# Two attentions and two feed-forwards on one core: second attention in the stage of its queries, rows moved sooner

## The chip, the cores and the metric

The kernel is one program for one core of a Trainium2 chip. The metric is the device time of an execution in microseconds (us), lower being better. All times below are of this one core. Its engines are TensorE (PE, with PEld for its weight loads), VectorE (DVE), ScalarE (ACT), GpSimd (POOL), and SyncE (SP), which here only issues transfers (DMA).

## What is computed

The reference runs two layers on `x` (8 batches, 112 rows, 512 wide) and a context of 8 x 375 rows:

```python
x = x + attention0(layernorm(x), context)     # one head, softmax(x c^T / sqrt(512)) c, masked
x = x + ffn0(layernorm(x))                    # rmsnorm, 8-bit activations, ternary w1, w2, w3, silu gate, 1408 wide
x = x + layernorm(Wo attention1(layernorm(x), context)) * gamma + beta   # 16 heads of 32, scaled
x = x + ffn1(layernorm(x))                    # integer weights 1408 wide with row scales, silu gate
```

The keys and values of attention1 are products of the context with `Wk` and `Wv` and hang on nothing of `x`. Products in f32 are made of two parts each (high and low), so every such product is three matmuls. The scores of attention1 are clipped to -50..50 (after the exponential, as a clip of `e`).

## The kernel before

All 896 rows are 7 tiles of 128 rows for the feed-forwards, and 8 batches of 112 rows for the attentions. The program is a row of blocks, one per stage; in each, every engine has its own list of instructions, written out by hand, and waits only on semaphores. Between two blocks stands a barrier: no engine begins the next block before all five have ended theirs.

- **First stage** (0 to 142 us): attention0 for each batch b, with the first 31 of 56 pieces of the keys and values of attention1 (`kv_product`, L161 to L180, pieces in the order k, k, v, k, v, k, v of each batch) woven between. SP stores every piece (`kv_spill`). For batch b, DVE's `add(b)` (L767) raises `x1_ready`, and SP's `move(b)` (L347) copies the 112 rows from `x` (by batch) to `xres` (by tile) with one or two DMAs. SP issues in order, so a move also waits for all that stands ahead of it. For b = 6 DVE's `tile_statistics(0)` (L441) waits until the rows of batches 0 to 5 have landed. The ternary form of w1 and w2 is made here by POOL (`scale_weight`, L322) and DVE (`ternary_weight`, L329 and L330); the last half of w2 is DVE's last work in this block.
- **Second stage** (142 to 271 us): ffn0 tile by tile with the other 25 pieces. It begins with the transposes of the first two tiles (`turn_input`, L1100), which share a PSUM bank, so that the second waits for ACT's copy of the first (L959). Three gate and up products (`gate_up`, L1109) per tile follow, with pieces 31 to 37 between those of tiles 0 and 1. ACT adds up |w3| in two halves (`sum_weight`, L301), PE totals them (`total_weight`, L308), DVE inverts, POOL scales, DVE rounds.
- **Queries** (the end of the same block, 264 to 297 us): seven transposed tiles, then `query(n, g)` (L1183): four groups g of heads for tiles 0 to 2 (n = 0) and for tiles 3 to 6 (n = 1), each 12 matmuls into the PSUM bank of its group (the same four banks for both n). ACT and DVE read it (L1061, L1340), and `q_lo` counts what DVE has done. `queries_stack(n)` (L877) waits for 4(n+1) of these and issues 8 DMAs which lay the queries of all heads in `qst`. Set 0 is stacked here, and SP waits for its landing before the block ends. The keys and values of batches 0 and 1 are fetched into `kst` and `vst` here too (L229, L234).
- **Second attention** (a block of its own, 297 to 395 us): `scores(m)` (L1617) for m = 0 to 31, which is group m % 4 of batch m // 4, 12 matmuls; ACT's exponential (L1574), DVE's clip (L1672), `values(b, g)` (L1631, L1634). PE works two groups of scores ahead of the values. SP begins with `queries_stack(1)`, then fetches the keys of batch b + 2 once the scores of batch b are done (`s_sum`), the values once its values are done. Scores of batch 3 and later need set 1 of the queries, the others set 0.
- **The rest** (398 to 517 us): ffn1 and the output.

## Time and profile before

| | us |
|---|---|
| three timed runs: median (lowest, highest) | 523.45 (521.83, 1657.42) |
| profiled execution, its time | 518.96 |
| its span, first to last instruction | 517.2 |
| TensorE busy in the span | 473.5 |
| VectorE, ScalarE, GpSimd busy | 293.4, 248.9, 84.0 |

The highest of the three is an outlier that nothing in the profile accounts for. All timeline numbers are microseconds from the start of the profiled execution's span; 1.8 us of its time lie outside the span. TensorE being busy 92% of the span makes every stop of it a candidate for the end, so a change is read off at the places where PE stands still.

### The profile page before, as it was taken

How to read it: one execution, taken by the hardware profiler on the slowest of the kernel's cores; microseconds unless marked ns; L12 is line 12 of the kernel's file. 1: busy time of each engine (PE TensorE's matmuls, PEld its weight loads, DVE VectorE, ACT ScalarE, POOL GpSimd, SP SyncE). 2: the span in 40 equal slices, each digit the busy share in tenths (PEclk: the TensorE clock that was granted, in tenths of full speed). 3: DMA queues.
4: the chain of work that ended last, by engine and by line, in shares of the span. 5: the costliest groups of instructions: out<-in, count | busy, mean ns of one | idle time of the engine just before them, and what ended most of it. 6: DMA issues, size and time to landing. Idle time of an engine off the chain costs nothing. (4 is left out here: it accounts for less than half of the span.)

```text
span 517.2 us, 10260 instructions
## 1 busy us (share of the span) xinstructions
PE 473.5 (92%) x4018; PEld 358.1 (69%) x4018; DVE 293.4 (57%) x554; ACT 248.9 (48%) x373; POOL 84.0 (16%) x105
## 2 busy tenths in 40 slices
PE   3899999999598799999997889999996998999997
PEld 3778888877376566666767677778874654555996
DVE  4674364428846956655564235668885686555211
ACT  4545433553357365666564287857761575112000
POOL 2210400024024000000108001133332116000000
PEclk9999999999979999999999989999999999999999
DMA  8989586923572113111127599777601546000011
GB/s 279 352 303 374 188 287 211 324 64 121 151 283 96 52 36 113 37 51 41 49 95 328 122 192 372 268 234 241 212 4 31 173 124 182 0 0 1 35 53 53
DMA packets 42716, 79.30 MB, mean 153 GB/s; under 512 B 5553, under 2 KB 30129, under 8 KB 40369
## 3 DMA queue, kind: packets, MB, share of 16 engines
q1 hardware_dynamic: 42672, 78.69, 46.1%
q8 instruction: 30, 0.49, 0.4%
q14 instruction: 12, 0.10, 0.0%
q10 hardware_dynamic: 2, 0.01, 0.0%
HBM read 58.76 MB, written 14.42 MB: 141 GB/s over the span
## 5 line engine op out<-in xcount | busy, mean ns | idle before, releaser
L179 PE MATMUL psum<-wv_p,kv_p 128*128 128x512 f32 x288 | 75.5, 411 | 6.5 <-DVE khl L199 5.1
L177 PE MATMUL psum<-kv_p,wk_p 128*128 128x384 f32 x384 | 75.8, 348 | 1.9 <-DVE khl L199 1.3
L177 PEld LDWEIGHTS psum<-kv_p,wk_p 128*128 128x128 f32 x384 | 68.3, 193 | 4.1 <-issue 2.9
L179 PEld LDWEIGHTS psum<-wv_p,kv_p 128*128 128x128 f32 x288 | 53.3, 188 | 23.1 <-issue 11.6
L1574 ACT ACTIVATE e<-psum,mask_bias 128x448 f32<-128x448 f32 x96 | 53.7, 636 | 14.8 <-PE psum L1617 14.6
L199 DVE SCALAR_TENSOR_TENSOR khl<-psum,bqk,khl 128x384 f16<-128x384 f32 x32 | 19.7, 616 | 44.0 <-ACT khl L189 43.9
L1844 PE MATMUL psum<-xt,wg_b 128*128 128x448 f16 x176 | 36.9, 352 | 3.1 <-DVEq L1919 3.1
L1631 PE MATMUL psum<-e,vst 128*32 128x112 f32 x768 | 37.7, 267 | 2.0 <-DVE e L1672 1.8
L1672 DVE TENSOR_SCALAR e<-e 128x1344 f32<-128x1344 f32 x32 | 28.2, 881 | 16.3 <-ACT e L1574 16.3
L1844 PE MATMUL psum<-xt,wu_b 128*128 128x448 f16 x176 | 36.9, 352 | 0.0
L1893 PE MATMUL psum<-h_p,wd_r 128*128 x176 | 36.0, 366 | 0.0
L193 ACT ACTIVATE vsp<-psum 128x512 f32<-128x512 f32 x24 | 14.3, 597 | 43.2 <-PE psum L179 42.9
L1893 PEld LDWEIGHTS psum<-h_p,wd_r 128*128 128x128 f32 x176 | 33.1, 188 | 2.7
L189 ACT ACTIVATE khl<-psum,bqk 128x384 f16<-128x384 f32 x32 | 18.4, 579 | 31.4 <-PE psum L177 31.4
L1790 ACT ACTIVATE gate<-psum,gs 128x448 f32<-128x448 f32 x22 | 13.9, 631 | 38.0 <-PE psum L1844 35.9
L1844 PEld LDWEIGHTS psum<-xt,wg_b 128*128 (+1 forms) x176 | 17.1, 98 | 18.6 <-issue 3.4
L322 POOL TENSOR_SCALAR w_stage<-w_stage,w_stat 128x2816 f32<-128x2816 f32 x6 | 16.4, 2738 | 80.8 <-DVE w_stat L317 80.7
L1907 DVE SCALAR_TENSOR_TENSOR hf<-psum,sgu,gate 128x448 f32<-128x448 f32 x22 | 15.0, 683 | 24.8 <-ACT gate L1790 24.8
L1617 PE MATMUL psum<-qst,kst 128*128 128x112 f16 x384 | 25.2, 215 | 3.8 <-PEq L1371 1.8
L1844 PEld LDWEIGHTS psum<-xt,wu_b 128*128 (+1 forms) x176 | 17.2, 98 | 16.1
L1617 PEld LDWEIGHTS psum<-qst,kst 128*128 128x128 f16 x384 | 20.0, 99 | 9.6 <-issue 5.8
L1634 PE MATMUL psum<-e,z_pick 128*32 128x112 f32 x512 | 25.1, 263 | 0.6 <-issue 0.6
(188 smaller groups left out, 834.7 us busy)
## 6 DMA issues: line engine op xcount, KB each, us to landing
kst<-k_scratch SPq DMA_DIRECT2D x8, 1536.0 KB, 8.2
kv_raw<-in_ctx_feat SPq DMA_DIRECT2D x12, 768.0 KB, 5.0
w_stage<-in_w SPq DMA_DIRECT2D x6, 1408.0 KB, 7.9
cn<-in_ctx_tok SPq DMA_DIRECT2D x8, 768.0 KB, 7.5
k_scratch<-khl SPq DMA_DIRECT2D x128, 48.0 KB, 1.7
v_scratch<-vsp SPq DMA_DIRECT2D x24, 256.0 KB, 2.2
vst<-v_scratch SPq DMA_DIRECT2D x8, 768.0 KB, 6.4
wd_int<-in_wd SPq DMA_DIRECT2D x11, 256.0 KB, 3.8
```

Of the source, the lines that this page charges most:

```text
L177: mm = pe.matmul(psum[:, kv_bank(p), 0:TP], wk_p[:, u, k, n * P:(n + 1) * P], src[:, v, k, :], **ends)
L179: mm = pe.matmul(psum[:, kv_bank(p), :], src[:, u, k, n * P:(n + 1) * P], wv_p[:, v, k, :], **ends)
L189: act.activation(khl[n][:, 0, :], psum[:, kv_bank(p), 0:TP], ACT.Identity, bias=bqk[:, 1, n:n + 1]).then_inc(kv_hi, 1)
L199: dve.scalar_tensor_tensor(khl[n][:, 1, :], psum[:, kv_bank(p), 0:TP], bqk[:, 1, n:n + 1], khl[n][:, 0, :], ALU.add, ALU.subtract).then_in ...
L322: pool.tensor_scalar(w_stage[:, w_half_of[half]], w_stage[:, w_half_of[half]], w_stat[:, 4 * n + 2:4 * n + 3], ROUND, ALU.mult, ALU.add).t ...
L1574: act.activation(e[g][:, c, :], psum[:, D_S + (TC * g + c) % 4, 0:4 * S], ACT.Exp, bias=mask_bias[:, b, c:c + 1]).then_inc(e_raw, 1)
L1617: mm = pe.matmul(psum[:, D_S + (TC * g + c) % 4, hh * S:(hh + 1) * S], kst[b % 2][:, g, hh, c * P:(c + 1) * P], qst[:, g, hh, b * S:(b + 1 ...
L1631: mm = pe.matmul(psum[32 * hh:32 * hh + 32, D_UZ[b][0], g * S:(g + 1) * S], vst[b % 2][:, c, (4 * g + hh) * HD:(4 * g + hh + 1) * HD], e[g ...
L1634: mm = pe.matmul(psum[32 * hh:32 * hh + 32, D_UZ[b][1], 0:S], (z_pick_last if c == TC - 1 else z_pick)[:, g, :], e[g][:, c, hh * S:(hh + 1 ...
L1672: dve.tensor_scalar(e[g][:], e[g][:], EXP_LOW, EXP_HIGH, ALU.max, ALU.min).then_inc(e_ready, 1)
L1844: mm = pe.matmul(psum[:, F_GU + 2 * q + m, 0:HALF], w[:, k, bass.ts(j, P)], xt[:, u, k, a * HALF:(a + 1) * HALF], start=(k, u) == (0, 0), ...
L1893: mm = pe.matmul(psum[:, F_D + m, 0:HALF], wd_r[:, j, m * P:(m + 1) * P], h_p[:, a, u, j, :], start=(j, u) == (0, 0), stop=(j, u) == (JC - ...
```

## The change

1. **First stage.** SP's `move(b)` stands ahead of the last pieces of batch b (`A_KV[b][2]`), no longer behind them at the start of batch b + 1. `ternary_weight(1, 1)` leaves the end of DVE's list and stands near the start of its list in the second block; PE's first `gate_up` waits for it, and so does SP's load of the second half of w3.
2. **Start of the second stage.** The second transpose has a bank of its own (`input_bank`) and waits for nothing of ACT. ACT's second `sum_weight` of w3 moves behind `square(0, 0)` and `normalized(6)`, PE's `total_weight` behind piece 34. DVE's and POOL's small steps around it change places, and one tiny scale of `row_scale` moves into `add`.
3. **Queries and second attention are one block.** The barrier between them goes. `query(1, 0)` and `query(1, 1)` use two other banks and wait for none of the first set's reads. `scores(0)` stands between `query(1, 1)` and `query(1, 2)`, `scores(1)` between `query(1, 2)` and `query(1, 3)`; `scores(0)` waits for the landing of stack 0, SP no longer does. ACT's exponentials and DVE's clips are woven in the same way. `wq_p1` moves to other memory so that `e` can be written earlier.

```diff
@@ first stage, SP, batch b
-                if b:
-                    move(sp, b - 1)
                 for p in A_KV[b][0]:
...
                     load_tok(b + 3)
+                move(sp, b)
                 for p in A_KV[b][2]:
@@ DVE, end of the first stage and start of the second
             input_integers(dve, 1)
-            ternary_weight(dve, 1, 1)
...
             gate_scales(1, 1)
+            ternary_weight(dve, 1, 1)
             keys_values((31,))
@@ second stage, PE
-                after(pe, xqt_ready, t)
+                after(pe, xqt_ready, t if t != 1 else 0)
...
             keys_values((31,))
+            pe.wait_ge(w_ternary, 4)
             gate_up(0, 0, 0)
@@ SP, end of the queries
             queries_stack(sp, 0)
-            sp.wait_ge(q_stacked[0], STACK)
+            queries_stack(sp, 1)
+            for b in range(B):
+                if b + 2 < B:
+                    sp.wait_ge(s_sum, TC * G * (b + 1))
+                    keys_fetch(sp, b + 2, b % 2)
...
@@ PE, queries and scores
-        C_T, C_Q = 0, 2
+        C_T, C_Q = 0, ((2, 3, 4, 5), (6, 7, 4, 5))
...
-                after(pe, q_lo, G * (n - 1) + g + 1)
+                if n == 1 and g < 2:
+                    pe.wait_ge(x2_ready, TILES + 1)
+                    kv_wait_read(pe, NP * B - 1)
+                if n == 1 and g >= 2:
+                    pe.wait_ge(q_lo, g + 1)
...
-            for g in range(G):
-                query(1, g)
+            query(1, 0)
+            query(1, 1)
+            scores(0)
+            query(1, 2)
+            scores(1)
+            query(1, 3)
@@ PE, scores(m), and values(b, g) for g == 0
-                    if b == 3:
-                        pe.wait_ge(q_stacked[1], STACK)
+                    if b in (0, 3):
+                        pe.wait_ge(q_stacked[b // 3], STACK)
+                if m < 2:
+                    pe.wait_ge(c_lo, TILES)
+                    pe.wait_ge(q_lo, m + 1)
...
+                    if b < 2:
+                        pe.wait_ge(ones_set, 6)
+                        pe.wait_ge(q_lo, G + 2 * (b + 1))
```

How the lists read at three places. First, SP in the first stage, batch 5 (`xres<-x` is the move of rows, `v_scratch` and `k_scratch` are pieces 23 and 24). Before:

```order
L208 DMA k_scratch<-khl_76 32x2x384 [waits kv_left]
L208 DMA k_scratch<-khl_76 32x2x384 x3
L211 DMA v_scratch<-vsp 128x512 [waits kv_hi]
L208 DMA k_scratch<-khl_77 32x2x384 [waits kv_left]
L208 DMA k_scratch<-khl_77 32x2x384 x3
L347 DMA xres<-x 80x512 [waits x1_ready]
L347 DMA xres<-x 32x512
```

Now:

```order
L208 DMA k_scratch<-khl_76 32x2x384 [waits kv_left]
L208 DMA k_scratch<-khl_76 32x2x384 x3
L347 DMA xres<-x 80x512 [waits x1_ready]
L347 DMA xres<-x 32x512
L211 DMA v_scratch<-vsp 128x512 [waits kv_hi]
L208 DMA k_scratch<-khl_77 32x2x384 [waits kv_left]
L208 DMA k_scratch<-khl_77 32x2x384 x3
```

The move of batch 5 has gone ahead of pieces 23 and 24, for which it had waited.

Second, ACT at the start of the second stage (`w3q,w_stat` is the second half of |w3|, `hy,hstat` the square of tile 0, `xn_b` a normalized tile, `khl` and `vsp` pieces 33 and 34). Before:

```order
L967 ACTIVATE silu_112<-psum,hstat 128x512
L301 ACTIVATE w3q,w_stat<-w_stage 128x2816
L458 ACTIVATE xn_b<-xres,bstat,rstd 128x512
L189 ACTIVATE khl_78<-psum,bqk 128x384
L967 ACTIVATE silu_111<-psum,hstat 128x384
L458 ACTIVATE xn_b<-xres,bstat,rstd 128x512
L974 ACTIVATE hy,hstat<-hid_105 128x1408
L193 ACTIVATE vsp<-psum 128x512
```

Now:

```order
L1151 ACTIVATE silu_112<-psum,hstat 128x512
L462 ACTIVATE xn_b<-xres,bstat,rstd 128x512
L189 ACTIVATE khl_78<-psum,bqk 128x384
L1151 ACTIVATE silu_111<-psum,hstat 128x384
L1158 ACTIVATE hy,hstat<-hid_105 128x1408
L462 ACTIVATE xn_b<-xres,bstat,rstd 128x512
L301 ACTIVATE w3q,w_stat<-w_stage 128x2816
L193 ACTIVATE vsp<-psum 128x512
```

The sum has moved from ahead of piece 33 to just ahead of piece 34's read; PE's total stands behind the product of piece 34.

Third, PE where the scores begin (`wq_p` and `xnt_p` are a query product, `qst,kst` scores). Before:

```order
L1183 MATMUL psum<-xnt_p_1615,wq_p_1611 128x512
L1371 UNCONDITIONAL_BRANCH
L1606 UNCONDITIONAL_BRANCH [waits barrier_Pool_Activation_PE_DVE_SP_release]
L1617 MATMUL psum<-qst,kst_80 128x112 [waits kst_loaded0]
L1617 MATMUL psum<-qst,kst_80 128x112 x15
```

Now:

```order
L1411 MATMUL psum<-xnt_p_1611,wq_p_1607 128x512
L1442 MATMUL psum<-qst,kst_80 128x112 [waits c_lo,q_lo,q_stacked0,kst_loaded0]
L1442 MATMUL psum<-qst,kst_80 128x112 x11
L1411 MATMUL psum<-xnt_p_1611,wq_p_1606 128x512 [waits hqt_ready,q_lo,c_lo,wq_lo]
L1411 MATMUL psum<-xnt_p_1611,wq_p_1606 128x512
```

The first scores stand in the middle of the query products, with a wait for stack 0 of their own, and the rest of the queries stands behind that wait.

## Rows read from the trace of the kernel before

**Rows 1.** The page: busy time of each engine.

```profile
PE 473.5 (92%) x4018; PEld 358.1 (69%) x4018; DVE 293.4 (57%) x554; ACT 248.9 (48%) x373; POOL 84.0 (16%) x105
```

**Rows 2.** Timeline, end of the first stage: start, us, work, [idle before <- what ended it].

```profile
106.97 0.75 DVE L767 SCALAR_TENSOR_TENSOR x<-psum,arow,x 112x512 f32<-112x512 f32 x1 [1.01 <-PE psum L703]
...
114.79 1.17 SPq L347 DMA_DIRECT2D xres<-x  x2
...
117.51 3.06 DVE L441 BATCH_NORM_STATS2 ln_stat<-xres 128x6 f32<-128x512 f32 x5 [4.24 <-DMA xres<-x]
...
128.11 2.32 PE L177 MATMUL psum<-kv_p,wk_p 128*128 128x384 f32 x12 [0.44 <-ACT vsp L193]
...
133.90 3.04 PE L179 MATMUL psum<-wv_p,kv_p 128*128 128x512 f32 x12 [0.90 <-DVE khl L199]
...
137.47 1.48 ACT L215 ACTIVATE kv_p<-kv_raw 128x1536 fp32r<-128x1536 f32 x1
138.40 0.54 DVE L482 TENSOR_SCALAR xs<-xres,ln_mv,bstat 128x512 f32<-128x512 f32 x1
...
140.97 0.89 DVE L330 TENSOR_SCALAR w2q<-w2q 128x2816 bf16<-128x2816 bf16 x1
```

**Rows 3.** Timeline, start of the second stage.

```profile
142.19 0.59 PE L1100 MATMUL psum<-ident_bf,xq 128*128 128x128 bf16 x4 [5.25 <-PEq L834]
...
143.89 4.00 PE L177 MATMUL psum<-kv_p,wk_p 128*128 128x384 f32 x12
...
154.86 2.54 ACT L301 ACTIVATE w3q<-w_stage 128x2816 bf16<-128x2816 f32 x1
...
159.47 3.04 PE L179 MATMUL psum<-wv_p,kv_p 128*128 128x512 f32 x12 [1.31 <-DVE khl L199]
...
160.80 2.63 POOL L322 TENSOR_SCALAR w_stage<-w_stage,w_stat 128x2816 f32<-128x2816 f32 x1 [5.66 <-DVE w_stat L317]
...
162.14 1.57 DVE L482 TENSOR_SCALAR xs<-xres,ln_mv,bstat 128x512 f32<-128x512 f32 x1
...
162.35 1.04 PE L1109 MATMUL psum<-w1q,xqt 128*128 128x512 bf16 x4
...
184.75 3.14 PE L179 MATMUL psum<-wv_p,kv_p 128*128 128x512 f32 x12
```

**Rows 4.** Timeline, queries and first scores (SPq: issue of a DMA).

```profile
284.27 11.15 PE L1183 MATMUL psum<-xnt_p,wq_p 128*128 128x512 f32 x48 [1.53 <-issue]
...
290.22 0.61 SPq L877 DMA_DIRECT2D qst<-qhl  x1
...
296.18 0.75 DVE L1340 SCALAR_TENSOR_TENSOR qhl<-psum,bqk,qhl 128x512 f16<-128x512 f32 x1 [1.97 <-ACT qhl L1061]
...
297.22 1.26 SPq L877 DMA_DIRECT2D qst<-qhl  x2
297.26 0.95 PE L1617 MATMUL psum<-qst,kst 128*128 128x112 f16 x16 [1.84 <-PEq L1371]
...
306.09 1.55 SPq L229 DMA_DIRECT2D kst<-k_scratch  x1
...
316.13 0.76 PE L1617 MATMUL psum<-qst,kst 128*128 128x112 f16 x12 [0.37 <-DMA kst<-k_scratch]
```

**Rows 5.** SP's waits, 280 to 300 us; landing of the key fetch of 306.09.

```profile
SPq L1371 <- DMA qst<-qhl: 3.2, 1, 3.2
...
kst<-k_scratch SPq DMA_DIRECT2D x1, 1536.0 KB, 10.0
```

**Rows 6.** Stretches: us, busy (count) of PE, PEld, DVE, ACT, POOL, clock, DMA, GB/s.

```profile
142.00:148.00 6.00, 5.04 (x22) 4.56 (x23) 0.21 (x2) 1.27 (x3) 0.00 (x0) 0.54 1.03 376
301.00:304.50 3.50, 3.35 (x60) 2.70 (x57) 1.89 (x3) 2.35 (x5) 0.00 (x0) 0.52 1.02 223
316.00:317.00 1.00, 0.87 (x20) 0.79 (x24) 0.75 (x1) 0.41 (x1) 0.00 (x0) 1.00 0.99 403
395.00:398.00 3.00, 0.01 (x1) 0.00 (x0) 2.44 (x5) 0.00 (x0) 0.10 (x1) 1.00 0.00 0
```

More of the change, by code:

```diff
@@ L1371, in build @@
-        part.close()
         e = [at(f"e{r}", [P, TC, 4 * S], F32, 56576 + r * 5376) for r in range(4)]
@@ new lines, in _ @@
+            turned_input(0, 0)
+            turned_input(1, 1)
+            keys_values((31,))
+            sum_weight(act, 2, 0)
+            gate(0, 0, 0)
+            keys_values((32,))
+            gate(0, 0, 1)
+            normalized(act, 5)
+            keys_values((33,))
+            gate(0, 0, 2)
+            square(0, 0)
+            normalized(act, 6)
+            sum_weight(act, 2, 1)
+            keys_values((34,))
+            gate(1, 1, 0)
+            scaled(0, 0)
+            keys_values((35,))
@@ new lines, in _, with tile_normalized @@
+            gate(1, 1, 1)
+            turned_input(2, 0)
+            keys_values((36,))
+            gate(1, 1, 2)
+            keys_values((37,))
+            turned_hidden(0)
+            keys_values(B_KV[0][0])
+            square(1, 1)
+            gate(2, 0, 0)
+            scaled(1, 1)
+            split_feat(act, B_SLOT[2], B_FILL[2])
+            for t in range(TILES - 2):
+                step(t, t % 2)
+            def tile_normalized(t):
+                act.wait_ge(b_shift, 3 if t < TILE_SETS[0][1] else 4)
+                after(act, c_turned, t - 1)
+                act.activation(xn_c[:, t % 2], xres[:, t, :], ACT.Identity, scale=rstd[:, t], bias=bstat[:, 7, t]).then_inc(c_xn, 1)
@@ new lines, in down, with step @@
+            def down(t):
+                pe.wait_ge(w_ternary, 6)
+                pe.wait_ge(hqt_ready, t + 1)
+                pe.wait_ge(x2_ready, t + 1)
+                for j in range(JC):
+                    mm = pe.matmul(psum[:, B_DN, :], hqt[:, j, :], w3q[:, j, :], start=j == 0, stop=j == JC - 1)
+                mm.then_inc(down_sum, 1)
+            def step(t, q):
+                gates, inputs = t + 2 < TILES, t + 3 < TILES
+                turn_hidden(t)
+                keys_values(B_KV[t][0])
+                if gates:
+                    gate_up(t + 2, q, 0)
+                down(t)
+                keys_values(B_KV[t][1])
+                if gates:
+                    gate_up(t + 2, q, 1)
+                if inputs:
+                    turn_input(t + 3)
+                keys_values(B_KV[t][2])
+                if gates:
+                    gate_up(t + 2, q, 2)
@@ new lines, in _, with turn @@
+            gate_up(1, 1, 2)
+            keys_values((37,))
+            for t in range(TILES - 1):
+                step(t, t % 2)
+            def turn(t):
+                pe.wait_ge(c_xn, t + 1)
+                pe.wait_ge(up_read, 3 * TILES)
+                after(pe, c_lo, t - 1)
+                if t == QT[0][1]:
+                    pe.wait_ge(kv_sum, NP * B)
+                for k in range(KC):
+                    mm = pe.transpose(psum[:, C_T + t % 2, k * P:(k + 1) * P], xn_c[:, t % 2, k * P:(k + 1) * P], ident[:])
+                mm.then_inc(c_turned, 1)
@@ L1608, in scores @@
+            turn_hidden(6)
+            keys_values(B_KV[6][0])
+            turn(0)
+            turn(1)
+            down(6)
+            turn(2)
+            turn(3)
+            query(0, 0)
+            turn(4)
+            query(0, 1)
+            query(0, 2)
+            turn(5)
+            query(0, 3)
+            turn(6)
             def scores(m):
```

793 lines of the change are left out of this document (353 added, 440 removed).

## The prediction, made before the changed kernel was run

> **What bounds the kernel now.** I read the page first: TensorE is busy for 473.5 of 517.2 us [rows 1], so 44 us are its stops, and only a stop, or TensorE's clock, can give or cost time. Then I read TensorE's timeline at the three places that the change touches, looking for each stop and for what ended it.
>
> At the end of the first stage TensorE has stopped at 136.94 (133.90 + 3.04) and begins again at 142.19, after 5.25 us [rows 2, 3]. The last engine to end that block is DVE, at 141.86 (140.97 + 0.89), with the ternary weights [rows 2]. DVE is late because it stood for 4.24 us until 117.51 for moved rows: the rows of batch 5 were ready at 107.72 (106.97 + 0.75), but their move was issued at 114.79 only [rows 2]. The same lag makes TensorE wait 0.44 and 0.90 us at 128.11 and 133.90 [rows 2].
>
> In the second stage the pieces and gate products are nearly dense; one stop of 1.31 us stands at 159.47, since ACT spent 2.54 us on |w3| ahead of piece 33 [rows 3].
>
> Between the queries and the scores TensorE stands for 1.84 us [rows 4] and then runs its first scores and values thinly, partly at the lower clock [rows 6]. This looks like the loss to remove. But the scores that begin at 316.13 (the first of batch 2) waited 0.37 us for their keys [rows 4]. So up to there the time is set by another chain: last query read by DVE at 296.93 (296.18 + 0.75), barrier, eight stack DMAs from 297.22, key fetch issued at 306.09, landed 10.0 us later, at 316.1 [rows 4, 5]. What TensorE does between is beside it.
>
> **The change part by part.** I write the new times on the clock of the old trace.
>
> *Rows sooner, first stage.* The move of batch 5 can be issued at 107.8 and lands by about 111 (the old one, issued at 114.79, had landed at 117.5 [rows 2]). DVE is ready for it at 113.27 (117.51 - 4.24). The 4.24 us go from DVE, though not all reach the stage's end, since some of its next steps wait for TensorE; I count 1.8 to 3.4 there. TensorE loses its two waits and ends piece 30 at 136.94 - 1.34 = 135.6.
>
> *The ternary half leaves the block.* DVE would end 2.54 us (1.65 + 0.89) sooner for that alone, at 139.4, and with the rows at 136.0 to 137.6. Now ACT is the last: its split of the next context began 0.53 us after TensorE's end and took 1.48, so it ends at 135.6 + 2.0 = 137.6 [rows 2]. With 0.3 for the barrier (141.86 to 142.19) the second stage begins at 138.0 to 138.2 in place of 142.19. I take -4.0; the ends are -1.9 (SP's last issues near 140.0 hold the barrier) and -5. The moved half costs 2.54 us of DVE in the next block, beside piece 31; TensorE's first gate product needs it 2.9 us in, and cannot start before 3 us in.
>
> *Start of the second stage.* The second transpose saves its wait of about 0.8 us. Piece 31 took 4.00 us at a granted clock of 0.54, that is mostly the lower one of 1.2 GHz [rows 3, 6]; a like piece at 2.4 GHz took 2.32 [rows 2]. If the shorter stop (2.4 us in place of 5.25) keeps the clock, another 1.7 us go. Counting on through gate products and pieces with the same durations, TensorE ends piece 34 at 16.3 us after its start. Here stands a new wait: the total of |w3|. ACT makes the square of tile 0 and a normalized tile first (until 16.9), then 2.54 us of sum and its read-out: 19.65. So TensorE stops for 3.3 us and its next gate product begins at 20.0, against 20.16 before (162.35 - 142.19). Then a shorter chain brings the two transposes' gain back, and DVE's third and fourth ternary steps, now later, hold piece 39: 40.4 against 42.56 (184.75 - 142.19). One thing eats of this: DVE's step at 162.14 took 1.57 us, ending 0.3 us after POOL's scaling of 160.80 to 163.43, where the same shape on its own took 0.54 [rows 2, 3]; now the rounding of tile 0 falls within POOL's second scaling, and waits some 1.3 us, which goes through to piece 36. I take -0.9; the ends are -2.2 (no such wait) and +1 (the clock stays low to piece 31).
>
> The Trainium skill (SBUF — State Buffer, "SBUF: two separate sides") says that VectorE and GpSimd share a port pair under an exclusive lock held for the whole instruction. The row at 162.14 agrees. Without the rule the sum would have -2.2 here in place of -0.9.
>
> *Queries and scores.* Up to query(1, 1) nothing changes: 284.27 plus half of 11.15 is 289.85. scores(0) then waits for stack 0. Its last DMA was issued at 290.22 and ended at 290.83, and SP waited 3.2 us more: landed at 294.0 [rows 4, 5]. So TensorE stops for 4.2 us, and the two last query products stand behind that wait. 0.76 of scores, 2.79, 0.76, 2.79: query(1, 3) ends at 301.1, ACT and DVE read it by 302.6 (0.7 + 0.75). Stack 1 hangs on this read and starts at 302.6 in place of 297.22: 5.4 us later. SP's queue behind it is as before, 8.9 us of issues and then the key fetch with 10.0 us. The keys land at 321.5 and scores of batch 2 begin 5.4 us later than before. The scores and values up to there run sooner, but only lengthen the stop ahead of it, to some 7 us. I take +5.4; the low end is +1.1 (were stack 0 there at 289.85, the two groups of scores alone delay the last query by 1.5, less 0.3 for the barrier), the high end is in the rivals.
>
> *The clock.* After 5.25 us of standing the clock was low [rows 3, 6]; after 3.05 us at 395 it was not (1.00), after the thin stretch from 295 it was, at 301 to 304.5 [rows 6]. The new stop of 7 us lies beyond the first case: I count 1.7 us, as piece 31 lost. The stop of 4.2 us lies between: 0.7 x 1.7 = 1.2, at the end of which every delay goes straight into the chain. For the 3.3 and the 2.4 us stops I count nothing.
>
> Behind batch 2 the order is the old one. The next keys were issued at 314.5 by the same queue and needed at 326.8; with all shifted they have more slack.
>
> Sum: -4.0 - 0.9 + 5.4 + 1.7 + 1.2 = +3.4. On the profiled execution's 518.96 that is 522.4, on the median of 523.45, which stands 4.5 above it (0.9%), 526.8. I predict 526.8.
>
> **The rivals.**
>
> *The attention gains what it shows.* If the chain of stack and keys had slack that I don't see, the merged block would give back its thin start: 1.84 of idle, some 2 us of thin scores and 1.1 of low clock (an estimate from 301 to 304.5 [rows 6]), 5 us. Then -4.0 - 0.9 - 5.0 = -9.9, and up to -12 with the clock kept in the second stage: 513.5 to 511.5. For it speak the idle rows; against it the 0.37 us wait at 316.13, which leaves no slack.
>
> *Clock.* TensorE falls to 1.2 GHz at each of the stops of 2.4, 3.3, 4.2 and 7 us. It decides if even the stop of 2.4 us ahead of the second stage brings the clock down. Against the sum that is 1.8 + 1.7 + 0.5 more: 530.8, slower than before by 7.4 us. For it speaks the thin stretch at 301, against it 395 to 398.
>
> *The key fetch shares.* Before, the values and `Wo` were issued 4.3 us behind the keys; now both stand ready behind them. If the three land together, 3.4 MB at the 403 GB/s of 316 us [rows 6] take 8.4 us. The last stack issue would end at 311.5 and land some 5 us later; the keys come at 325.0, 3.5 later: 530.3. The Trainium skill (DMA: Bandwidth & Descriptors, "Two DMAs through the same engine are not ordered") says that descriptors of one queue start in order, which speaks against it.
>
> *Rows sooner does nothing.* The barrier stays at 140 for SP's issues: -1.9 for -4.0, 528.9.
>
> **How the numbers follow.** The forecast (all within 3 us of 526.8) gets 0.43, the gaining attention 0.12, the clock 0.20, the sharing 0.12, the barrier 0.08, the rest 0.05. A measurement of this kernel tells about 2% (10.5 us) from no change. Below 513.0 lies a part of the first rival only, 0.05; above 533.9 clock and sharing together, 0.07; within 0.88. The range for 8 in 10 goes from 518, where the gaining attention meets the forecast's low end, to 533, where clock and sharing meet.
>
> **What would show it.** In the changed profile: DVE's wait for `xres` gone, and the second stage starting near 138.0; a stop of some 3.3 us at the total of |w3|, released by ACT; a stop near 4 us at the first scores, released by a DMA; stack 1 issued over 5 us later against query(1, 0), and a stop of about 7 us at the first scores of batch 2, released by `kst`, with the clock below 1.00 behind it. I am wrong if scores(0) finds stack 0 landed, if the keys of batch 2 are waited for less than 3 us, or if the first stage ends later than 140.

## The result and the profile after the change

The changed kernel takes 526.16 us (median of 6 runs, 524.31 to 527.22) and the kernel before, run beside it, 522.41 us. The ratio is 1.0084, with a 95% interval of 1.0048 to 1.012: slower by 2.5 to 6.3 us, 4.4 in the middle, and less than the 2% below which the prediction calls a difference no change. The profiled execution has a span of 524.9 us, 7.7 more than that of before. Why the profiles differ by more than the medians is part of the reading below.

The page, where [rows 1] stood before:

```profile
PE 479.4 (91%) x4018; PEld 362.1 (69%) x4018; DVE 292.7 (56%) x554; ACT 248.4 (47%) x373; POOL 82.5 (16%) x105
```

TensorE is busy for 5.9 us more with the same 4018 matmuls. Nothing was added to its work, so it ran some of it at the lower clock.

Timeline of the changed kernel at the end of its first stage, for [rows 2]:

```profile
107.42 0.75 DVE L769 SCALAR_TENSOR_TENSOR x<-psum,arow,x 112x512 f32<-112x512 f32 x1 [1.01 <-PE psum L705]
...
108.20 1.17 SPq L347 DMA_DIRECT2D xres<-x  x2
...
113.64 3.05 DVE L445 BATCH_NORM_STATS2 ln_stat<-xres 128x6 f32<-128x512 f32 x5
...
125.80 4.41 PE L177 MATMUL psum<-kv_p,wk_p 128*128 128x384 f32 x24
...
136.11 1.48 ACT L215 ACTIVATE kv_p<-kv_raw 128x1536 fp32r<-128x1536 f32 x1
...
137.78 0.61 SPq L211 DMA_DIRECT2D v_scratch<-vsp  x1
...
138.89 1.01 PE L1323 MATMUL psum<-ident_bf,xq 128*128 128x128 bf16 x8 [3.31 <-PEq L835]
```

The rows of batch 5 are moved 0.78 us after their addition began, where it was 7.8 us, and DVE's wait of 4.24 us for them is gone. TensorE's two small waits are gone too: what stood as two groups of 12 with 0.44 us between them is one of 24. The last to end the stage is SyncE, with a spill that ends at 138.39. The second stage starts 31.47 us after the addition of batch 5 began (138.89 - 107.42), where it was 35.22.

Start of the second stage, for [rows 3]:

```profile
156.24 2.53 ACT L301 ACTIVATE w3q<-w_stage 128x2816 bf16<-128x2816 f32 x1
...
158.92 0.81 PE L308 MATMUL psum<-w_stat,ones_f 128*128 128x1 f32 x4 [2.98 <-ACT w3q L301]
...
159.59 1.87 PE L1332 MATMUL psum<-w1q,xqt 128*128 128x512 bf16 x4
...
160.22 5.21 POOL L322 TENSOR_SCALAR w_stage<-w_stage,w_stat 128x2816 f32<-128x2816 f32 x2 [2.83 <-DVE w_stat L317]
...
161.25 1.70 PE L1332 MATMUL psum<-w2q,xqt 128*128 128x512 bf16 x4
...
165.20 0.97 DVE L1535 TENSOR_SCALAR hq<-hy 128x1408 bf16<-128x1408 f32 x1 [0.70 <-ACT hy L1163]
```

The new stop at the total of |w3| is there, 2.98 us long and ended by ScalarE. The gate product behind it takes 1.87 us, where a like one took 1.04 [rows 3].

Queries and first scores, for [rows 4]:

```profile
280.54 5.78 PE L1411 MATMUL psum<-xnt_p,wq_p 128*128 128x512 f32 x24 [1.53 <-issue]
...
290.28 1.28 PE L1442 MATMUL psum<-qst,kst 128*128 128x112 f16 x12 [3.96 <-issue]
...
291.33 5.03 PE L1411 MATMUL psum<-xnt_p,wq_p 128*128 128x512 f32 x12
...
300.55 0.75 DVE L1635 SCALAR_TENSOR_TENSOR qhl<-psum,bqk,qhl 128x512 f16<-128x512 f32 x1 [1.00 <-ACT qhl L1245]
...
310.64 0.66 SPq L229 DMA_DIRECT2D kst<-k_scratch  x1
...
319.02 1.30 PE L1442 MATMUL psum<-qst,kst 128*128 128x112 f16 x12 [5.99 <-DMA kst<-k_scratch]
```

Before, four query products ran as one row of 48 matmuls in 11.15 us. Now two run, TensorE stops for 3.96 us at scores(0), and the third product takes 5.03 us in place of 2.8. The last query is read at 301.30, that is 20.76 us after query(1, 0) began (12.66 before); the keys are issued 30.10 us after it (21.82 before); the scores of batch 2 begin 38.48 us after it (31.86 before), behind a stop of 5.99 us.

Stretches, for [rows 6] (us, busy (count) of PE, PEld, DVE, ACT, POOL, clock, DMA, GB/s):

```profile
160.00:164.00 4.00, 4.00 (x16) 2.32 (x15) 0.37 (x2) 0.97 (x2) 3.78 (x2) 0.68 0.79 262
290.00:294.00 4.00, 3.72 (x18) 3.21 (x19) 0.86 (x1) 1.68 (x3) 0.00 (x0) 0.50 0.00 0
316.00:324.00 8.00, 4.98 (x92) 4.39 (x96) 0.86 (x1) 2.41 (x5) 0.00 (x0) 0.57 1.01 421
440.00:442.00 2.00, 2.00 (x7) 0.89 (x6) 0.60 (x1) 0.00 (x0) 1.10 (x2) 0.50 0.72 217
```

Behind each of the stops of 2.98, 3.96 and 5.99 us the clock was at 1.2 GHz (0.50) for a while: 0.50 is that level, 0.68 and 0.57 are stretches of which it fills a part. One more such stretch, at 440, stands in the last stage, which the change does not touch, and another at the product that starts that stage, behind a stop as long as before:

```profile
401.97 3.12 PE L1844 MATMUL psum<-xt,wg_b 128*128 128x448 f16 x8 [3.06 <-DVEq L1919]
...
437.67 0.66 PE L998 MATMUL psum<-ident,xn_e 128*128 128x128 f32 x4 [2.16 <-ACT xn_e L975]
...
438.60 2.73 PE L1844 MATMUL psum<-xt,wg_b 128*128 128x448 f16 x8
```

In the profile of before that product began at 398.06 behind a stop of 3.05 us, took 1.67 us, and from 398 to 402 the clock was 1.00. From there to the end before took 119.1 us (517.2 - 398.06) and the changed kernel 122.9. So 3.8 of the 7.7 us between the two spans come from a stage with the same code. They can be told apart row by row: the first product is 1.45 us longer; behind the stop of 2.16 us (1.59 before) the two products that start at 438.60 (gate and up) take 4.71 us until the next begins, where the same two took 3.02; and that stop itself is 0.57 us longer. That is 3.1 us of lower clock and 0.6 of a longer wait.

### The profile page after: what moved, and what is told of

Same layout as the page of the kernel before. It is cut to its first block and busy times, and to the rows that moved or that the text cites. A ratio compares the mean times of both kernels' runs of the same rounds, so it can differ in the third digit from the quotient of the medians.

```text
span 524.9 us, 10260 instructions
## 1 busy us (share of the span) xinstructions
PE 479.4 (91%) x4018; PEld 362.1 (69%) x4018; DVE 292.7 (56%) x554; ACT 248.4 (47%) x373; POOL 82.5 (16%) x105
## 5 line engine op out<-in xcount | busy, mean ns | idle before, releaser
L1844 PE MATMUL psum<-xt,wg_b 128*128 128x448 f16 x176 | 39.4, 370 | 3.1 <-DVEq L1919 3.1
L1667 DVE TENSOR_SCALAR e<-e 128x1344 f32<-128x1344 f32 x32 | 28.2, 881 | 22.4 <-ACT e L1276 22.4
L1515 DVE SCALAR_TENSOR_TENSOR hid<-psum,bstat,silu 128x512 f32<-128x512 f32 (+1 forms) x21 | 14.8, 704 | 20.9 <-ACT silu L1151 20.6
```

Source lines behind the costliest of these rows:

```text
L1667: dve.tensor_scalar(e[g][:], e[g][:], EXP_LOW, EXP_HIGH, ALU.max, ALU.min).then_inc(e_ready, 1)
L1844: mm = pe.matmul(psum[:, F_GU + 2 * q + m, 0:HALF], w[:, k, bass.ts(j, P)], xt[:, u, k, a * HALF:(a + 1) * HALF], start=(k, u) == (0, 0), ...
```

## The experiments

Three times cut the span into what each part of the change can reach: from the addition of batch 5 to the second stage, from there to query(1, 0), and from there to the first gate product of the last stage. They are differences of starts in TensorE's timeline of each profile (the addition of batch 5 in DVE's). All ratios are to the kernel before, run beside, and a time in us that goes with one is worked out from it. Rows of one column with the same code show how far single profiles scatter: 30.5 to 31.9 us in the first (ten profiles with the changed first stage), 140.4 to 141.7 in the second (eight with the changed order there), 113.4 to 114.1 in the third (three with the order of before).

| kernel | to second stage | to query(1, 0) | to last stage | ratio (95%) |
|---|---|---|---|---|
| before | 35.22 | 142.08 | 113.79 | 1 |
| changed | 31.47 | 141.65 | 121.43 | 1.0084 (1.0048 to 1.012) |
| moves alone | 32.48 | 142.50 | 113.37 | 0.9927 (0.989 to 0.9964) |
| first part alone | 30.46 | 142.69 | 114.12 | 0.9939 (0.9908 to 0.997) |
| third part alone | 35.21 | 142.30 | 121.97 | 1.0195 (1.0156 to 1.0234) |
| changed, old order of the second stage | 31.85 | 140.99 | 122.42 | 1.0077 (1.005 to 1.0103) |
| changed, scores behind the queries | 31.03 | 140.58 | 113.78 | 0.9915 (0.9886 to 0.9944) |
| changed, scores one product later | 31.72 | 141.68 | 116.12 | 0.9983 (0.9952 to 1.0013) |
| changed, stop of scores(0) filled | 31.11 | 140.44 | 119.24 | 1.0045 (1.0021 to 1.0069) |
| changed, stacks from two queues | 30.71 | 140.37 | 125.76 | 1.0163 (1.0112 to 1.0215) |
| scores behind, keys ahead of stack 1 | 31.20 | 140.59 | 121.83 | 1.0145 (1.008 to 1.021) |
| scores behind, last-stage stop filled | 31.13 | 141.69 | 113.75 | 0.989 (0.9865 to 0.9916) |
| the same, stop at the total filled too | 31.43 | 141.62 | 113.82 | 0.9921 (0.9894 to 0.9948) |
| before, last-stage stop filled | 35.24 | 142.42 | 113.00 | 0.9985 (0.996 to 1.0011) |

### The three parts, one at a time

The first part alone, on the kernel before:

```diff
-                if b:
-                    move(sp, b - 1)
                 for p in A_KV[b][0]:
...
+                move(sp, b)
                 for p in A_KV[b][2]:
...
-            ternary_weight(dve, 1, 1)
...
             gate_scales(1, 1)
+            ternary_weight(dve, 1, 1)
...
+            pe.wait_ge(w_ternary, 4)
             gate_up(0, 0, 0)
```

> The kernel before with the first part of the change alone: moves issued a step sooner, the last ternary half in the next block. My theory: the second stage starts near 138.5 in place of 142.19 and nothing later takes this back, so the kernel is 3.3 to 4.0 us faster (ratio 0.9925 to 0.9937). Rival (a later wait takes it back, as DVE holds piece 32 for the ternary half, or the queries wait for wq or POOL): the second stage starts as soon, but query(1, 0) leads by under 1.5 us, and the ratio is 0.997 to 1.000.

Measured: by the ratio 3.2 us faster (1.6 to 4.8). That is just under the 3.3 that I expected at least. Query(1, 0) begins 173.15 us behind the addition of batch 5 in place of 177.30 (the first two columns), 4.15 us sooner, and up to the last stage only 0.3 us of it is lost. The rival, which gave query(1, 0) a lead under 1.5 us, falls.

The moves alone, without the ternary half:

```diff
-                if b:
-                    move(sp, b - 1)
                 for p in A_KV[b][0]:
...
+                move(sp, b)
                 for p in A_KV[b][2]:
```

> The kernel before with the moves of the rows issued a step sooner, alone; the last ternary half stays at the end of the first stage. My theory: DVE's wait of 4.24 us for the rows is gone and TensorE's waits of 0.44 and 0.90 us with it, but DVE still ends the stage with the ternary half, 1.8 to 3.4 us sooner, and the second stage starts 2.0 to 3.5 us sooner against the addition of batch 5 (35.22 us behind it before, 31.7 to 33.2 now, against some 31.5 with both edits); ratio 0.993 to 0.997. Rival (the moves are of no use alone, as TensorE and the spills hold the end): the second stage starts less than 1 us sooner, ratio 0.998 to 1.001.

Measured: 3.8 us faster (1.9 to 5.7), a little more than I expected, and the second stage 32.48 us behind the addition. The moves alone gave 2.74 us at the second stage's start. The ternary half, which in this kernel still ends its block, gives the rest: 1.0 us against the changed kernel, 2.0 against the first part alone, and 1.3 against the mean of the ten profiles that have both (timeline of the kernel with the moves alone):

```profile
138.13 0.89 DVE L330 TENSOR_SCALAR w2q<-w2q 128x2816 bf16<-128x2816 bf16 x1
...
139.35 0.59 PE L1098 MATMUL psum<-ident_bf,xq 128*128 128x128 bf16 x4 [4.32 <-PEq L832]
```

In the time of the whole kernel the ternary half cannot be seen: the intervals of the two kernels overlap.

The third part alone (the joined block of queries and second attention with the scores between the query products, as in the change, and the two other parts undone, but for the tiny scale that moved into `add`):

> The kernel before with the third part of the change alone: one block of queries and second attention, the first scores between query products. My theory: batch-2 scores begin 6.6 us later against query(1, 0), and the lower clock behind the stop costs 1.5 to 2 more: 8 to 8.6 us slower than the kernel before (ratio 1.0153 to 1.0165). Rival (the parts do not add up: the joined block costs only what the sooner first stage shifts): 3 to 5 us slower.

Measured: 10.2 us slower (8.1 to 12.2), with 8.2 us between query(1, 0) and the last stage. That is my theory's side, at the edge of its numbers. The rival falls. The first and third part together give 7.0 us where the whole change gives 4.4; with intervals of 1.6 and 2.1 us on the two this is no contradiction, and I do not read a gain of the second part from it.

The second part undone in the changed kernel, but for the second transpose's own bank and the scale in `add`:

```diff
             gate_up(0, 0, 2)
-            keys_values((34,))
             total_weight(pe, 2, B_DN)
+            keys_values((34,))
```

with ScalarE's, DVE's and GpSimd's order of before at that place too.

> The changed kernel with the order of the kernel before at the start of the second stage: |w3| summed and totalled ahead of piece 34, rounding and rows in the old places; all else as changed. My theory, from the trace: the new order brought about 0.4 us (41.70 against 42.56 us from the stage's start to piece 39, part of it by the second transpose's own bank, which stays), so this kernel is within 1 us of the changed one, at +4 to +5 us on the kernel before; the stop of 2.98 us at the total is gone and others stand in its place. Rival (the stop of 2.98 us and the clock behind it are a pure loss): 3 to 4.5 us faster than the changed kernel, level with the one before.

Measured: 525.22 us, 4.0 us slower than before, as the changed kernel is. In place of the stop of 2.98 us stands a wait of 1.31 us at piece 34, for DVE. The new order is worth nothing that can be measured, and the longer stop that it brings is no loss either. The pair of fillers below shows why.

### The place of the scores

The changed kernel with its scores behind the last query product:

```diff
             query(1, 1)
-            scores(0)
             query(1, 2)
-            scores(1)
             query(1, 3)
+            scores(0)
+            scores(1)
```

and the same for the exponentials and the clips.

> The changed kernel with the first two groups of scores behind the last query product instead of between the query products, in one block still. My theory (the stop for stack 0 stands ahead of the query products on which stack 1 hangs): no stop for stack 0 is left, or under 1 us, stack 1 is issued 16.6 us or so after query(1, 0) starts in place of 20.7, the batch-2 scores begin some 6 to 7 us sooner against query(1, 0), and the kernel is 7.5 to 9 us faster than the changed one, 3.5 to 5 us faster than the one before (ratio 0.990 to 0.993). Rival (the joined block itself costs, by another order of queues or the clock): not over 3 us faster than the changed kernel.

Measured: 517.02 us, 4.4 us faster than before (2.9 to 5.9) and by the ratios 8.8 faster than the changed kernel. Timeline of this kernel:

```profile
279.36 11.33 PE L1411 MATMUL psum<-xnt_p,wq_p 128*128 128x512 f32 x48 [1.53 <-issue]
...
292.23 8.96 SPq L878 DMA_DIRECT2D qst<-qhl  x8
...
301.23 1.39 SPq L229 DMA_DIRECT2D kst<-k_scratch  x1
...
311.11 0.76 PE L1442 MATMUL psum<-qst,kst 128*128 128x112 f16 x12 [1.65 <-DMA kst<-k_scratch]
```

No stop is left at the first scores, which follow the last query product; stack 1 begins 12.87 us after query(1, 0), sooner than the 16.6 of my expectation, which I had put too late; the batch-2 scores begin 31.75 us after it, in place of 38.48. So the block may be joined without loss, and what cost was the place of the two groups of scores. Joining by itself gains almost nothing: 113.78 us to the last stage against 113.79.

One product later each (scores(0) behind query(1, 2), scores(1) behind query(1, 3)):

> The changed kernel with scores(0) behind query(1, 2) and scores(1) behind query(1, 3), one product later each. My theory (the stop for stack 0 is 3.96 us less what stands ahead of it, and a short stop costs no clock): the stop at scores(0) is 1.0 to 1.4 us, query(1, 3) runs at 2.4 GHz and ends some 13.3 us after query(1, 0) starts in place of 19.1, stack 1 and the keys of batch 2 move with it, and the kernel is 5.5 to 7.5 us faster than the changed one, 1.5 to 3 us slower than the one without scores between the products (ratio to the kernel before 0.994 to 0.998). Rival (one product is as good as two: the clock falls at the short stop too): query(1, 3) takes 5 us, and the gain is 3 to 3.5 us.

```profile
289.23 0.75 PE L1442 MATMUL psum<-qst,kst 128*128 128x112 f16 x12 [1.07 <-issue]
289.80 3.02 PE L1411 MATMUL psum<-xnt_p,wq_p 128*128 128x512 f32 x12
```

These rows of its timeline show the stop shrunk to 1.07 us and the product behind it at full clock, ending 13.2 us after query(1, 0) began. By the ratios it is 5.3 us faster than the changed kernel, just under the 5.5 that I expected at least. The stop ahead of the keys of batch 2 is still 4.32 us long, and their scores begin 33.71 us after query(1, 0). In three kernels the stop at scores(0) ends 9.6 to 9.7 us after query(1, 0) began (changed 9.74, this one 9.62, the next 9.69), whatever TensorE did until then. The profile puts this stop down to nothing (`issue`), but the landing of stack 0 fits it: in the changed kernel its eight issues run from 279.94 to 286.79, the shortest of its DMAs took 3.5 us to land, and scores(0) began at 290.28.

The stop of scores(0) filled with work of no use (16 products into the bank that query(1, 2) overwrites):

```diff
             query(1, 1)
+            pe.wait_ge(q_lo, 3)
+            for n in range(16):
+                pe.matmul(psum[:, 4, :], wq_p[0][:, 0, 0:P], xnt2_p[1][:, 0, 0, :], start=True, stop=True)
             scores(0)
```

> The changed kernel with 16 matmuls of 128x512 without use ahead of scores(0), written to the bank that query(1, 2) overwrites: the stop of 3.96 us is filled with some 3.7 us of work, nothing else is moved. My theory (the lower clock behind that stop is on the path): granted clock 1.00 behind it, query(1, 2) takes 2.8 us in place of 5.03, scores(0) 0.76 in place of 1.28, stack 1 and the batch-2 scores come 2.5 to 2.9 us sooner against query(1, 0), and the kernel is 2.5 to 3 us faster than the changed one (ratio to before 1.002 to 1.005). Rival (the clock falls for another reason than the stop, or its cost is hidden in the stop for the keys): the clock is 0.5 all the same or the batch-2 scores do not move, and the gain is under 1 us.

```profile
283.74 3.80 PE L1479 MATMUL psum<-xnt_p,wq_p 128*128 128x512 f32 x16
287.81 0.75 PE L1442 MATMUL psum<-qst,kst 128*128 128x112 f16 x12 [0.27 <-issue]
288.38 3.02 PE L1411 MATMUL psum<-xnt_p,wq_p 128*128 128x512 f32 x12
...
314.57 1.30 PE L1442 MATMUL psum<-qst,kst 128*128 128x112 f16 x12 [6.49 <-DMA kst<-k_scratch]
```

and its stretch behind the filler:

```profile
288.00:292.00 4.00, 4.00 (x37) 3.29 (x35) 0.86 (x1) 2.25 (x4) 0.00 (x0) 1.00 0.00 0
```

With the stop filled the clock stays at 2.4 GHz, scores(0) takes 0.75 in place of 1.28 us and query(1, 2) 3.02 in place of 5.03. The batch-2 scores come 2.03 us sooner against query(1, 0) (36.45 against 38.48), and the kernel is 2.0 us faster by the ratios, whose intervals overlap. So, by the profile, the clock behind that stop costs some 2 us of the 4.4. That is a little less than the 2.5 to 3 us I gave it, and on the path, as the batch-2 scores moved with it.

### Two ways round SyncE's queue that failed

Half of each stack's DMAs from ScalarE's queue:

```diff
-            queries_stack(sp, 0)
-            queries_stack(sp, 1)
+            queries_stack(sp, 0, (0,))
+            queries_stack(sp, 1, (0,))
...
             turned_hi(6)
+            act.wait_ge(kv_sum, NP * B)
+            queries_stack(act, 0, (1,))
...
             query_hi(1, 3)
+            queries_stack(act, 1, (1,))
```

> The changed kernel with four of the eight DMAs of each query stack issued from ScalarE's queue, beside SyncE's four; the scores stay between the query products. My theory (what is late is not the data but SyncE's eight issues of 0.6 to 1.1 us one behind another): stack 0 lands 3 to 3.5 us sooner, the stop at scores(0) is under 1 us with the clock at 1.00, the key fetch of batch 2 is issued some 9 us sooner, and the kernel is 8 to 10.5 us faster than the changed one (ratio to before 0.988 to 0.993). Rival (ScalarE pays for it: its four issues ahead of the exponentials of group 2 take 3.5 to 4 us, which TensorE's values wait for): 5 to 7 us faster than the changed one, and a stop of 3 to 4 us at the first values.

Both ranges fell: by the ratios it is 4 us slower than the changed kernel. The cost that the rival named is there, at twice its size, and the gain that both counted on is not. Its timeline:

```profile
277.62 6.31 ACTq L878 DMA_DIRECT2D qst<-qhl  x4
...
288.16 1.28 PE L1445 MATMUL psum<-qst,kst 128*128 128x112 f16 x12 [4.14 <-issue]
...
299.45 7.86 ACTq L878 DMA_DIRECT2D qst<-qhl  x4
...
307.36 3.25 ACT L1278 ACTIVATE e<-psum,mask_bias 128x448 f32<-128x448 f32 x6 [8.72 <-issue]
...
308.05 1.08 PE L1445 MATMUL psum<-qst,kst 128*128 128x112 f16 x8 [7.94 <-ACT e L1278]
...
309.16 0.54 SPq L229 DMA_DIRECT2D kst<-k_scratch  x1
```

and what its issues took (ns, min/median/max):

```profile
L878 ACTq DMA_DIRECT2D qst<-qhl x8: 641/1821/2657, 277.6 to 304.7; - x8
L878 SPq DMA_DIRECT2D qst<-qhl x8: 604/1044/2482, 277.6 to 302.2; - x8
```

In the changed kernel the 16 issues of SyncE alone have a median of 802 ns, and the first eight are done in 6.85 us. From two queues at once, ScalarE's four took 6.31 us and SyncE's four 5.05, and scores(0) began 9.92 us after query(1, 0), no sooner than in the changed kernel. For stack 1 the issues ended after 7.86 us in place of 9.27. Against these 0.5 and 1.4 us ScalarE stood still: 8.72 us ahead of its exponentials, for which TensorE's scores waited 7.94 us. The keys of batch 2 in turn wait for those scores, and were issued 30.9 us after query(1, 0) (30.1 in the changed kernel). That the two queues share something that makes the transfers fits the longer issues, but no run separates it. The Trainium skill (DMA: Bandwidth & Descriptors, "Issuing engines are not separate DMA queues") says that issuing from several engines at once saves only the time to initiate the DMA on the sequencer. These rows show little even of that: half of the issues moved away saved 0.5 of 6.85 us.

Keys, values and `Wo` ahead of stack 1, on the kernel with the scores behind the queries:

```diff
-            queries_stack(sp, 1)
             for b in range(B):
...
                 if b == 0:
                     sp.dma_start(wk_raw[:], wo).then_inc(proj_loaded[0], 16)
+                    queries_stack(sp, 1)
```

> As the kernel without scores between the products, and SyncE issues the keys, the values and Wo behind batch 0 ahead of the eight DMAs of stack 1. My theory (the keys of batch 2 hang on stack 1 only by the order of one queue): keys issued 2.4 us sooner, the stop of 1.65 us at the batch-2 scores is gone, and stack 1 lands some 36 us after query(1, 0) starts, ahead of the batch-3 scores at 38: 1 to 2 us faster than that kernel, ratio to before 0.987 to 0.990. Rival (stack 1 behind 3.3 MB of fetches lands too late): a stop of 2 to 6 us at the scores of batch 3 instead, level with that kernel or up to 4 us slower.

The batch-2 scores come 28.4 us after query(1, 0) (3.3 us sooner), and no stop is put down to stack 1. Yet the last stage comes 8.05 us later than without the edit. Its four runs go from 520.42 (the profiled one) to 530.52 us, all above the seven without the edit (517.75 at most), so that it is slower is clear and by how much is not: 12 us by the ratios, 3.4 by the spans of the two profiles. The profile has a stop where neither theory had one (timeline, then stretches):

```profile
309.20 0.38 PE L1459 MATMUL psum<-e,vst 128*32 128x112 f32 x8
314.93 0.60 PE L1462 MATMUL psum<-e,z_pick 128*32 128x112 f32 x8 [5.36 <-issue]
```

```profile
308.00:312.00 4.00, 1.57 (x44) 1.22 (x37) 1.72 (x2) 1.95 (x4) 0.00 (x0) 1.00 0.99 285
312.00:316.00 4.00, 1.07 (x24) 0.94 (x23) 0.00 (x0) 0.00 (x0) 0.00 (x0) 0.62 1.12 208
```

TensorE stands for 5.36 us in the middle of one group of values, between two matmuls with no wait between them, while the DMA engines are full (0.99 to 1.12). It fits an engine whose next instructions came late behind the fetches: the only transfer of instructions from 308 to 316 us ran from 312.2 to 313.5, inside the stop. But no run tried this, and it stays open. A second cost can be read: the key fetch issued behind stack 1 at 314.02 took 14.2 us to land, and TensorE waited 2.00 us for it.

### The clock in the last stage and at the total

Nine products of no use behind the last product of the second attention's block, on the kernel with the scores behind the queries:

```diff
             project(pe, 4)
+            pe.wait_ge(e_raw, TC * G * B)
+            for n in range(9):
+                pe.matmul(psum[:, D_S, :], ctxt_p[0][:, 0, 0, :], wo_p[:, 0, 0, :], start=True, stop=True)
```

> As the kernel without scores between the products, with 9 matmuls of 128x512 without use behind the last product of the second attention's block, written to a bank of scores already read: they fill some 2 of the 3.06 us for which TensorE stands ahead of the first gate product of the last stage. My theory (that stop brings the clock down in most executions: 0.50 to 0.60 behind it in four of five profiles, 1.00 in the profile of the kernel before): granted clock 1.00 behind it, the first gate product takes 1.68 us in place of 3.1, and the kernel is 1 to 2 us faster than the one without the filler (ratio to before 0.987 to 0.990). Rival (the profiles' clocks there are chance and the mean cost is small, or the filler delays the barrier): within 0.5 us of it, 0.9905 to 0.993.

```profile
394.68 1.67 PE L1847 MATMUL psum<-xt,wg_b 128*128 128x448 f16 x8 [1.02 <-DVEq L1922]
```

The stop is 1.02 us and the product behind it takes 1.67 us in place of 3.14, so the clock was kept. The kernel takes 515.59 us, ratio 0.989 (0.9865 to 0.9916), the best of all: 5.7 us faster than before and some 1.3 faster than without the filler. Its interval and that of the kernel without the filler overlap, so the 1.3 us alone are likely, not shown. (The profile shows 1.5 us at this product.)

With the stop at the total of |w3| filled too:

```diff
             keys_values((34,))
+            pe.wait_ge(up_read, 2)
+            for n in range(12):
+                pe.matmul(psum[:, B_GU + 2, :], xqt[0][:, 0, :], w1q[:, 0, 0:512], start=True, stop=True)
             total_weight(pe, 2, B_DN)
```

> As the last one, with 12 more matmuls of 128x512 without use ahead of the total of |w3|, in the bank that the next gate product overwrites: they fill 2.5 of the 2.98 us stop there. My theory (that stop costs clock too, the gate product behind it took 1.87 in place of 1.04 us): the clock behind the total is 1.00, piece 39 ends 1.3 to 2 us sooner against the stage's start, and the kernel is 1.3 to 2 us faster than the last one (ratio to before 0.984 to 0.987). Rival (pieces behind the stop wait for other engines, so the clock costs nothing): level with the last one within 0.5 us.

My theory falls: nothing is gained. By the ratios the kernel is even 1.6 us slower than with the one filler, but the intervals overlap. Its timeline shows what takes the clock's place:

```profile
158.96 1.02 PE L1332 MATMUL psum<-w1q,xqt 128*128 128x512 bf16 x4
...
159.59 5.24 POOL L322 TENSOR_SCALAR w_stage<-w_stage,w_stat 128x2816 f32<-128x2816 f32 x2 [2.63 <-DVE w_stat L317]
...
163.11 2.47 DVE L1541 TENSOR_SCALAR hq<-hy 128x1408 bf16<-128x1408 f32 x1 [0.70 <-ACT hy L1163]
...
166.25 1.97 PE L177 MATMUL psum<-kv_p,wk_p 128*128 128x384 f32 x10 [1.35 <-DVE khl L199]
```

Behind the filled stop the gate product is back at 1.02 us. DVE's rounding of tile 0 now comes 1.6 us sooner against the stage's start (24.75 against 26.31), falls within GpSimd's scaling (until 164.83), and takes 2.47 us where it took 0.97; piece 36 waits 1.35 us for what is queued behind it. So one price stands in for the other: piece 39 begins 41.63 us into the stage with this stop filled, and 41.70 in the changed kernel and 41.71 with the one filler, where it is not.

These three profiles can be compared because they agree in one more thing, which the table hides. In the same code, piece 31 ran at the lower clock in some profiles and not in others:

```profile
139.66 3.45 PE L177 MATMUL psum<-kv_p,wk_p 128*128 128x384 f32 x12
```

in the changed kernel (behind a stop of 3.31 us), and in the one with the scores behind the queries (behind 2.87 us):

```profile
139.19 2.33 PE L177 MATMUL psum<-kv_p,wk_p 128*128 128x384 f32 x12
```

Of the nine profiles in which each of the two transposes has its own bank, four kept the clock there (stops of 2.55 to 3.04 us) and reach query(1, 0) after 140.4 to 140.6 us; of the five that lost it (2.97 to 3.69 us), the four with the new order reach it after 141.6 to 141.7.

The same nine products in the kernel before:

> The kernel before with the same 9 matmuls behind the last product of the second attention's block. My theory (its runs spread over 6 us because the clock behind the 3.05 us stop ahead of the last stage falls in some executions and not in others): 1 to 2 us faster than the kernel before (ratio 0.996 to 0.998) and its slowest run under 523. Rival (the spread has other causes): ratio 0.9985 to 1.001 and the same spread.

Measured: 0.8 us faster at best guess (ratio 0.996 to 1.0011), with runs from 518.83 to 524.24 us. The spread stays. The mean granted clocks of the 22 runs of the kernel before beside it go only loosely with their times: the slowest, 526.98 us, has the lowest (0.977), but one of 518.98 us and one of 524.35 us have the same 0.987. So the clock at the start of the last stage is not what spreads the runs of the kernel before by 6 us, or not it alone. My theory falls there, and the cause of the spread stays open.

## Why the prediction was right, and where its sizes were not

The forecast of 526.8 us stands against 526.16 measured, +3.4 us against +4.4 (2.5 to 6.3). That the times agree better than the changes is luck: the base of 523.45 was the median of three runs, that of six is 522.41. The likeliest mechanism was the one that came, and several of its sizes were off, in ways that cancel, which is luck too.

**First stage, -4.0.** Measured -3.75 in the changed kernel. DVE's wait went, TensorE's two waits went, and piece 30 ended 28.2 us behind the addition of batch 5, where 28.6 was said. The step that failed is who is last: I took ScalarE's split, and it was SyncE with its last spill, 0.8 us later. The rival in which SyncE holds the barrier until 140 is out. (141.86 less 2.54 is 139.3, where the prediction has 139.4; nothing hangs on it.)

**Start of the second stage, -0.9.** Measured -0.86 to piece 39 (180.59 - 138.89 = 41.70 against 42.56), of which 0.4 is left at query(1, 0). The stop at the total was 2.98 us for 3.3. But the term's number is luck. Its count took piece 31 at the full clock, and in this profile the clock fell there, 1.1 us; the profiles that kept it reach piece 39 after 40.4 to 40.6 us, that is -1.9 to -2.2. I counted no clock behind the stop at the total either, and it cost 1.5 us on the two gate products behind it (1.87 and 1.70 in place of 1.04 and 1.03). Against both, I counted 1.3 us for DVE behind GpSimd's scaling, and hardly any of it came (0.97 us for the rounding, 0.89 before), as TensorE's delay had moved the rounding to the end of the scaling. With that stop filled, the wait that I had predicted is there, 1.5 us long. The Trainium skill (SBUF — State Buffer, "SBUF: two separate sides") has this lock between VectorE and GpSimd last for the whole instruction; the row at 163.11 ends 0.75 us behind GpSimd's, and agrees.

**Queries and scores, +5.4.** The stop of 4.2 us was 3.96. The keys were issued 8.3 us later against query(1, 0), not 5.4: most of the difference is the clock behind the stop, which I had at 1.2 us, in a term of its own, and which was 2.2 on query(1, 2) and 0.5 on scores(0). Against this the fetch landed 8.3 us after its issue, where it took 10.0 before [rows 5]:

```profile
kst<-k_scratch SPq DMA_DIRECT2D x1, 1536.0 KB, 8.3
```

Together 6.62 us at the batch-2 scores, where 5.4 and 1.2 make 6.6. The sum was right because an undersized clock and an oversized landing met. The landing also ends the rival in which the key fetch shares with the values and `Wo` queued behind it: they were issued 0.7 and 1.7 us behind the keys, and the keys came sooner, not later. What the Trainium skill says on it (DMA: Bandwidth & Descriptors, "Two DMAs through the same engine are not ordered"), that descriptors of one queue start in order, is not contradicted.

**Clock behind the long stop, +1.7.** The stop was 5.99 us for 7 and the clock fell (0.57 from 316 to 324). From the batch-2 scores to the last stage it took 82.95 us in place of 81.93, so 1.0 us.

**The clock rival (530.8).** It was nearer than its chance of 0.20 says: the clock fell behind all four stops, the one ahead of the second stage among them (3.31 us long for 2.4; piece 31 took 3.45 us, between 2.32 and 4.00). The step that failed is the one that took a stop of about 3 us as safe. It rested on one stop of one profile; the row given for it, 395 to 398, is that stop itself, and the product behind it did run at full clock (1.67 us), but in seven of eleven profiles it did not. What kept the sum is that behind 2.98 us the price displaced another wait, and ahead of the second stage it was 1.1 for 1.7.

**The gaining attention** is out: the joined block gains 0.0 us to the last stage even with its scores at the best place, because the chain through stack 1 and the key fetch sets the time, as [rows 4] showed with its wait of 0.37 us.

**Behind the prediction's terms**, -3.75 - 0.43 + 7.64 = +3.5 us come from the three stretches of the table. Of the rest of the 7.7 us between the profiles, 3.8 are in the last stage (3.1 of it clock) and 0.45 ahead of the addition of batch 5. I read the profile of before as typical there (1.00 behind a stop of 3.05 us). Of the eleven profiles with that stop unfilled, four kept the clock (before, the moves alone, the filled scores(0), the keys ahead of stack 1) and seven lost it.

## What to carry to other kernels

Before you move work into a gap, find the operand that comes last for it and what is queued behind the place where it would wait: scores(0) was ready for its bank and its keys, and stood for the stack, with the query products that feed the next stack behind it. The same two groups of scores one place later cost 5 us less, and behind the last query product 9 us less. Where a profile shows idle time and beside it a chain that makes TensorE wait 0.4 us at its end, the idle time is not the loss.

## What the runs showed of the hardware

- A stop of TensorE near 3 us may or may not cost the clock, in the same code: behind the stop of 3.05 to 3.08 us ahead of the last stage the first product took 1.67 us in the profile of before and 3.12 us in that of the changed kernel. Over eleven profiles of eleven kernels it was lost in seven. The length of the stop alone does not tell: ahead of the second stage the clock was kept behind stops of 2.55 to 3.04 us in four profiles, and low behind 2.97 to 3.69 in five and, with the order of before, behind 2.31 (0.50 over the 5.5 us from that start); in the last stage of the changed kernel it fell behind 2.16. Work of no use in a stop kept the clock each time it was tried, and paid only where no other wait stood behind it: 2.03 us at scores(0) in the profile, likely 1.3 us ahead of the last stage in the joined kernel, nothing at the total of |w3|.
- DMAs of many small rows issued from ScalarE and SyncE at the same time took 1.8 and 1.0 us each (medians) where SyncE alone took 0.8: two queues did not make the stack land sooner, and each issue held ScalarE.
- A stop of 5.36 us in the middle of a group of matmuls without waits, while the DMA engines were full (busy share 0.99 to 1.12). Its cause is open.
